# Second edge stage of a two-layer graph network: destination rows by spans of ranks instead of gathers

## What is computed

```
ms = src_s[edge_src] + dst_s[edge_dst]          # 64 scalars
mv = src_v[edge_src] + dst_v[edge_dst]          # 32 vectors of 3
w  = radial(edge_scalars) @ rw3 + roff          # 224 weights an edge, w1..w5
ds = [w1 * ms, w4 * (mv . Y1)]
dv = [(w2 * ms) Y1, w3 * mv, w5 * cross(mv, Y1)]
ls, lv = linear(ds), linear(dv)                 # 8 heads
a  = softmax over the edges of one destination of the heads' logits
ns, nv = segment sums of a * values by edge_dst
```

## Time and profile before

| | |
|---|---|
| median of 3 runs | 10502.52 us (10501.54 to 10524.19) |
| the profiled execution's own time | 10505.42 us |
| its span, first to last instruction | 10503.6 us |
| mean granted TensorE clock | 0.923 of full speed |
| PE, DVE, ACT, POOL busy over the span | 82%, 76%, 45%, 73% |
| layer1_edges, first to last sum (line 1849) | 5637.8 to 9768.5 us |

### The profile page before, as it was taken

One profiled execution on the slowest core, in us unless ns is written; L12 is line 12 of the kernel. 1 busy time (PEld: TensorE's weight loads), 2 busy tenths in 40 slices (PEclk: granted clock), 3 DMA queues, 4 the chain that ended last, 5 costly groups with the idle time before them and its releaser, 6 DMA issues. The chain is left out here.

```text
span 10503.6 us, 169632 instructions
## 1 busy us (share of the span) xinstructions
PE 8641.0 (82%) x31592; PEld 4931.7 (47%) x31592; DVE 7996.0 (76%) x15399; ACT 4717.1 (45%) x8484; POOL 7636.1 (73%) x5822
## 2 busy tenths in 40 slices
PE   0888888888888799999996888888888887788598
PEld 0444444444444232223233666666666665566333
DVE  3277777777777587888886888888888888888565
ACT  0177666666666311111112444444444444444255
POOL 4488888888888787777785777777777777777332
PEclk9599999999999899999997999999999999999699
DMA  5588888888888899999993444444444444444222
GB/s 202 177 169 168 166 167 166 169 164 172 165 167 168 180 231 225 228 226 229 228 226 90 136 138 136 135 133 139 136 135 135 136 140 135 133 135 137 71 76 58
DMA packets 1075659, 1661.68 MB, mean 158 GB/s; under 512 B 215917, under 2 KB 815288, under 8 KB 1019704
## 3 DMA queue, kind: packets, MB, share of 16 engines
q1 hardware_dynamic: 679744, 1199.16, 41.6%
q0 software_dynamic: 395520, 458.93, 24.5%
HBM read 1483.21 MB, written 443.97 MB: 183 GB/s over the span
## 5 line engine op out<-in xcount | busy, mean ns | idle before, releaser
L436 POOL DMA_INDIRECT sums<-e_total,e_place x1568 | 2481.9, 1583 | 586.3 <-DMA sums<-e_total,e_place 315.7
L1837 POOL DMA_INDIRECT e_rows<-TS,e_at x1568 | 1644.3, 1049 | 567.7 <-issue 451.4
L1837 POOL DMA_INDIRECT e_rows<-TD,e_at x1568 | 1537.3, 980 | 478.0 <-issue 478.0
L573 PE MATMUL ps<-e_win,e_pick 128*128 128x448 f32 x3136 | 1350.6, 576 | 152.9 <-DVE e_u L470 112.4
L1997 PE MATMUL ps<-w_r,e_h 128*128 128x224 f32 x3136 | 840.5, 420 | 424.6 <-DVE e_d L1880 376.1
L573 PEld LDWEIGHTS ps<-e_win,e_pick 128*128 128x128 f32 x3136 | 626.4, 205 | 920.0 <-issue 835.5
L1086 POOL TENSOR_TENSOR n_zv<-n_zv,n_ast 128x1536 f32<-128x1536 f32 x200 | 755.3, 3776 | 410.2 <-DMA n_zv<-in_x_groups 399.3
L1997 PEld LDWEIGHTS ps<-w_r,e_h 128*128 128x128 f32 x3136 | 659.2, 221 | 682.7 <-DVE e_d L1880 558.1
L2006 PE MATMUL ps<-ident,e_d 128*128 128x128 f32 x4704 | 683.6, 283 | 110.1 <-ACT e_dT L2114 108.6
L1266 PE MATMUL ps<-n_z,w_uss 128*64 128x512 f32 x1600 | 742.2, 607 | 26.5 <-DVE n_z L1109 25.8
L2114 ACT ACTIVATE e_oT<-ps 128x512 f32<-128x512 f32 x784 | 468.3, 597 | 628.3 <-PE ps L2032 488.5
(11 more groups left out here) (433 smaller groups left out, 18808.0 us busy)
## 6 DMA issues: line engine op xcount, KB each, us to landing
e_win<-T SPq DMA_DIRECT2D x1568, 168.0 KB
n_z<-in_x_groups SPq DMA_DIRECT2D x400, 512.0 KB
n_zv<-in_x_groups SPq DMA_DIRECT2D x800, 192.0 KB
TOT<-e_tot SPq DMA_DIRECT2D x392, 352.0 KB
e_row<-in_src_rows SPq DMA_DIRECT2D x98, 1024.0 KB
e_row<-in_dst_rows SPq DMA_DIRECT2D x98, 1024.0 KB
e_win<-T SPq DMA_DIRECT2D x1568, 56.0 KB
e_local<-LR SPq DMA_DIRECT2D x98, 512.0 KB
```

The lines of the kernel that those rows point to most:

```text
L436: pool.indirect_dma_start(sums[c], bass.IndirectOffsetOnAxis(ap=place[:, r % 4, c:c + 1], axis=0), total[:, r % 4, c, 0:MSG0], None, compu ...
L573: pe.matmul(g[:, c, :], pick[:, p, R * c:R * c + R], win[:, s, c, :], start=True, stop=True).then_inc(spread, 1)
L1837: pool.indirect_dma_start(rows[:, p, x, c, :], None, table, bass.IndirectOffsetOnAxis(ap=at[:, gp, x, col:col + 1], axis=0)).then_inc(rows ...
```

## The change

TD's rows are stored by rank, and layer1_edges reads them as layer0_edges reads T0: one window of 32 ranks a tile, or of 128 where the flag says so, spread to the edges by a matmul with a 0/1 selection, and copied from PSUM to the place in `rows` that the gather filled. Part by part:
- `edge_ranks` also writes first ranks and flags to a DRAM table BASE (one transfer); `node_ranks` clears 128 rows behind TD.
- `node_update0`: SyncE stores only TS; GpSimd copies four columns of ranks and issues two indirect scatters to TD behind each of the parts 6 and 7 of a group (100 in all).
- `layer1_edges`, GpSimd: four gathers a step instead of eight.
- SyncE: load_windows(i+4) ahead of each step's other work: 8 register loads and 8 transfers (4 of them conditional); every fourth step load_base and load_local (512 KB, LR to all partitions).
- VectorE: selections(i+3) as the last instruction of a step; sums waits for far_kept.
- TensorE: spread_out(i+2) in two halves, each of two matmuls with 160 columns, ahead of the halves of turn_back(i-1); turn_back comes ahead of weights(i+1).
- ScalarE: keep_far(i+2), two copies of 128x320, ahead of all else in a step.

The core of the diff:

```
-def layer1_edges(nc, m, k, ps, W, TS, TD, index, dstI, rows_dst, heads_dst, H, yx, TOT):
+def layer1_edges(nc, m, k, ps, W, TS, TD, index, LR, BASE, iota, dstI, rows_dst, heads_dst, H, yx, TOT):
...
         def bank(i, j):
-            return 2 + (5 * i.r + j) % 2
+            return 2 + (7 * i.r + j) % 2
...
+                def load_windows(i):
...
+                    for c in range(GT):
+                        sp.dma_start(win[0:FEW, s, c, :], TD[bass.ds(starts[c], FEW), :]).then_inc(win_here[s], 16)
+                        sp.dma_start(win[FEW:128, s, c, :], TD[bass.ds(starts[c] + FEW, 128 - FEW), :], cond=more[c]
+                                     ).then_inc(win_here[s], 16)
...
-                        for x, table in enumerate((TS, TD)):
-                            for c in range(GT):
-                                col = 4 * (r % 4) + c
-                                pool.indirect_dma_start(rows[:, p, x, c, :], None, table, bass.IndirectOffsetOnAxis(
-                                    ap=at[:, gp, x, col:col + 1], axis=0)).then_inc(rows_here[p][x], 16)
+                        for c in range(GT):
+                            col = 4 * (r % 4) + c
+                            pool.indirect_dma_start(rows[:, p, 0, c, :], None, TS, bass.IndirectOffsetOnAxis(
+                                ap=at[:, gp, col:col + 1], axis=0)).then_inc(rows_here[p], 16)
...
+                    dve.tensor_scalar(pick[:, p, :], local[:, gp, GT * R * s:GT * R * s + GT * R], iota[:, 0:1], None,
+                                      ALU.is_equal).then_inc(picked, 1)
...
                         if not i.before(5):
                             members(i)
+                        if i.plus(3).within():
+                            selections(i.plus(3))
...
+                def spread_out(i, half, to, after):
+                    p, s = i.r % 2, i.r % 4
+                    if half == 0:
+                        gate(pe, k)
+                        pe.wait_ge(picked, i.n(1, 1))
+                        gate(pe, k)
+                        pe.wait_ge(win_here[s], i.uses(256, 128 * (i.r // 4) + 128))
+                    if after is not None:
+                        gate(pe, k)
+                        pe.wait_ge(*after)
+                    for c in (2 * half, 2 * half + 1):
+                        last = pe.matmul(to[:, c % 2], pick[:, p, R * c:R * c + R], win[:, s, c, :], start=True, stop=True)
+                    last.then_inc(spread, 1)
...
+                        if i.plus(2).within():
+                            spread_out(i.plus(2), 0, far2(i, 0), (far_kept, 3) if i.before(1) else (kept, i.n(5, -1)))
+                        if not i.before(1):
+                            turn_back(i.plus(-1), 0)
+                        if i.plus(2).within():
+                            spread_out(i.plus(2), 1, far2(i, 1), (far_kept, 4) if i.before(1) else (kept, i.n(5)))
+                        if not i.before(1):
+                            turn_back(i.plus(-1), 1)
                         if not (isinstance(t, int) and t == PASSES - 1 and r == STEPS - 1):
                             weights(after)
-                        if not i.before(1):
-                            turn_back(i.plus(-1), 0)
-                            turn_back(i.plus(-1), 1)
...
+                def keep_far(i, half, of):
+                    gate(act, k)
+                    act.wait_ge(spread, i.n(2, half + 1))
+                    if half == 0 and not i.before(2):
+                        gate(act, k)
+                        act.wait_ge(added, i.n(1, 1, 2))
+                    act.activation(rows[:, i.r % 2, 1, 2 * half:2 * half + 2, :], of, ACT.Copy).then_inc(far_kept, 1)
...
                         i = At(t, r)
+                        if i.plus(2).within():
+                            keep_far(i.plus(2), 0, far2(i, 0))
+                            keep_far(i.plus(2), 1, far2(i, 1))
                         if r % 4 == 1 and not i.before(5):
                             weigh_up(i)
                         if not i.before(1):
```

In node_update0:

```
-                    for j, to in enumerate((TS, TD)):
-                        sp.dma_start(to[at, :].rearrange("(t n) w -> n t w", t=2), rows[:, r, :, X * j:X * j + X]
-                                     ).then_inc(stored[r], 16)
+                    sp.dma_start(TS[at, :].rearrange("(t n) w -> n t w", t=2), rows[:, r, :, 0:X]).then_inc(stored[r], 16)
...
+                    for j in range(2):
+                        pool.indirect_dma_start(TD, bass.IndirectOffsetOnAxis(ap=rank_of[:, c.p, 2 * r + j:2 * r + j + 1], axis=0),
+                                                rows[:, r, j, X:2 * X], None).then_inc(placed[r], 16)
...
+                        if s >= 6 and not g.before(1):
+                            place(g.plus(-1), s - 6)
```

More of the change, by code:

```diff
@@ L160, in _, with edge_ranks @@
                 dve.wait_ge(cast, len(casts))
-def edge_ranks(nc, m, k, ps, dstI, before, lower, LR, baseI):
+def edge_ranks(nc, m, k, ps, dstI, before, lower, LR, baseI, BASE):
     own = ExitStack()
@@ L230, in _, with node_ranks @@
                                    ).then_inc(kept, 1)
-def node_ranks(nc, m, k, ps, P, lower, nodes, T0):
+def node_ranks(nc, m, k, ps, P, lower, nodes, T0, TD):
     own = ExitStack()
@@ L940, in groups, with node_update0 @@
         body(Group(0, 0).plus(i))
-def node_update0(nc, m, k, ps, W, xT, xG, sums, X1, TS, TD):
+def node_update0(nc, m, k, ps, W, xT, xG, sums, X1, TS, TD, rank):
     own = ExitStack()
@@ L960, in node_update0 @@
         rows = sb("n1_rows", [128, 2, 2, 2 * X])
+        rank_of = sb("n1_rank_of", [128, 2, 4], I32)
+        ranked, begun = sem("n1_ranked"), sem("n1_begun")
+        placed = [sem(f"n1_placed{r}") for r in range(2)]
         x_here, ag_here = [sem(f"n1_x_here{p}") for p in range(2)], sem("n1_ag_here")
@@ L1090, in vectors, with ranks, place @@
                         pool.tensor_tensor(zv[:, b, 0], zv[:, b, 0], zv[:, b, i], ALU.add).then_inc(zv_ready, 1)
+                def ranks(c):
+                    if not c.before(2):
+                        for r in range(2):
+                            gate(pool, k)
+                            pool.wait_ge(placed[r], c.n(32, 0, 1))
+                    pool.tensor_copy(rank_of[:, c.p], rank[:, bass.ds(c.n(4), 4)]).then_inc(ranked, 1)
+                def place(c, r):
+                    gate(pool, k)
+                    pool.wait_ge(rows_kept, c.n(2, r + 1))
+                    gate(pool, k)
+                    pool.wait_ge(ranked, c.n(1, 1))
+                    pool.sem_inc(begun, 1)
+                    gate(pool, k)
+                    for j in range(2):
+                        pool.indirect_dma_start(TD, bass.IndirectOffsetOnAxis(ap=rank_of[:, c.p, 2 * r + j:2 * r + j + 1], axis=0),
+                                                rows[:, r, j, X:2 * X], None).then_inc(placed[r], 16)
                 def body(g):
@@ L1096, in body @@
                             add_up(g.plus(1))
+                        if s == 4 and not g.before(1):
+                            ranks(g.plus(-1))
+                        if s >= 6 and not g.before(1):
+                            place(g.plus(-1), s - 6)
                 add_up(Group(0, 0))
                 groups(pool, body)
+                ranks(Group(NG // 2, 0))
+                for r in range(2):
+                    place(Group(NG // 2, 0), r)
             @block.vector
@@ L1787, in body @@
                     for r in range(STEPS):
-                        i = At(t, r)
+                        i, ahead = At(t, r), At(t, r).plus(4)
+                        if ahead.within():
+                            gate(sp, k)
+                            sp.wait_ge(spread, ahead.n(2, 2, 4))
+                            load_windows(ahead)
+                        if r % 4 == 0 and not final:
+                            load_base(r // 4, t + 1)
+                        if r % 4 == 1 and not final:
+                            gate(sp, k)
+                            sp.wait_ge(picked, i.n(1, 3))
+                            load_local(r // 4, t + 1)
                         if not (final and r >= 6):
@@ L1809, in _ @@
                 for p in range(2):
+                    load_base(p, 0)
+                    load_local(p, 0)
                     load_at(p, 0)
                     load_h(p, 0)
+                sp.wait_ge(blank, 1)
+                for r in range(4):
+                    load_windows(At(0, r))
                 for p in range(2):
@@ L1975, in _ @@
                 dve.wait_ge(ones_set, 2)
+                for r in range(3):
+                    selections(At(0, r))
                 sums(At(0, 0))
@@ L1998, in weights @@
                     last.then_inc(w_ready, 1)
+                def spread_out(i, half, to, after):
[11 more added lines that the diff above has]
+                    last.then_inc(spread, 1)
                 def turn(i, j):
                     p = i.r % 2
```

(19 more changed lines are left out.)

84 lines of the change are left out of this document (64 added, 20 removed).

## The result

The changed kernel takes 10873.17 us (median of 4 runs, 10863.72 to 10891.59), the kernel before beside it 10502.03 us (4 runs, 10497.09 to 10524.19): ratio 1.0356, 95% interval 1.0332 to 1.0379, slower by 371 us. The profiled execution took 10891.59 us with a span of 10889.8, 386.2 us more than the span before.

The account below looks back on a forecast made before the run. GpSimd's gather queue was taken as the limit, VectorE close behind. New waits make a group 44.6 us against 42.3, +226 us; node_update0 +10 and prologue +5 give +241, forecast 10745 us, range 10420 to 10950.

Parts of the forecast that it names:

- the forecast's own case: Whole kernel: slower through new waits in the second edge stage, 10680 to 10880 us, chance 0.42.
- rival 4: Behind the scans TensorE stays at its lower clock, or SyncE binds: +400 to +600 us, 10900 to 11100; chance 0.11.
- What bounds before, the floor: Second edge stage: GpSimd's queue sets the pace by a little; without other VectorE waits a changed group takes 40.4 us.
- plain step: Second edge stage, VectorE step without scans or new wait: 9.00 us plus a selection of 0.48, 9.48 us.
- The scan step: Second edge stage, one step in four: forward scan waits 1.06 us for logits_up, so the step takes 12.98 us.
- The step behind the scans, order: ScalarE's Exp and table loads stand behind keep_far: 2.54 us of new VectorE wait, step 12.02 us.
- P: The end of VectorE's selection, which releases TensorE's spreads; VectorE starts its next step then too.
- The step behind the scans, clock: TensorE, idle some 3.5 us, may run at its lower clock: 0 to 1.2 us a group, 0.6 taken.
- node_update0: Four scatters a group of 512 nodes, covered by GpSimd's waits for transfers: +10 us taken, 125 without cover.
- The rest: BASE and the longer prologue: 0 to 15 us, 5 taken.
- SyncE: Windows and register loads in the edge stage: 0 taken, upper bound 0.7 us a step, 270 us.
- rival 5: Selections and gathers exclude each other, 0.95 us lost a selection: 372 us more, 11120 us; chance 0.02.

Follow-up runs that it names:

- e5: The kernel before without its gathers of destination rows, nothing in their place: 10224.03 us, beside the kernel before at 12677.2 us.
- e4: The changed kernel with selections first on VectorE, and Exp and turned-back results ahead of the spread rows: 10419.26 us, ratio to the kernel before 0.9927.
- e6: The changed kernel with five unread matmuls added on TensorE behind the logits' weighting: 10750.87 us, ratio to the kernel before 1.0235; 11400.18 under the other condition.
- the last two sets: Two of four sets of experiment runs, each with the kernel before alongside; there it took 10506.19 and 10503.86 us.
- the first two: The two earlier sets of experiment runs, each with the kernel before alongside; there it took 12677.2 and 12687.29 us.
- e1: The changed kernel with the selection for step i+3 moved from last to first in VectorE's step: 10589.76 us, ratio 1.0082; 10876.67 under the other condition.
- e3: The changed kernel with selections first on VectorE and Exp ahead of ScalarE's two copies: 10458.96 us, ratio 0.9955; 10791.59 and 10785.89 under the other condition.
- the first set: The earliest of four sets of experiment runs, four altered kernels with the kernel before alongside at 12677.2 us.

## Why the prediction was right, and where its size was off

Slower was forecast with 0.70, at 10745 us (+241 on the profiled execution), and 10873 us was measured (+386 by the spans): the forecast's own case, at its upper end (10680 to 10880), just short of rival 4, the clock (10900 and more). By its own steps:

- **What bounds before, the floor.** GpSimd's queue was the limit by a little: confirmed in that with half of the gathers VectorE waits for no row, and e5, the kernel before with that alone changed, has a group of 39.3 us instead of 42.2. The floor of 40.4 us a group stands: e4 has 40.3 in the second group of a pass. The terms are right to 0.1 us (plain step 9.48 forecast, 9.38 measured, as a selection costs 0.40 from start to start, not its duration of 0.48).
- **The scan step.** Forecast 12.98 us with 1.06 of wait for logits_up; measured 13.09 with 1.05. But only in the second group of each pass (33 waits in 65 groups): in the first VectorE itself comes 1.3 us late to the pass ("issue"), and the step is 11.97. The forecast counted this wait for all 98 groups; that the late start fills its place in the other 49 is luck.
- **The step behind the scans, order.** Forecast without the clock: results at P + 6.25, step 12.02. e6, which has TensorE at full clock, has P + 6.52 and 12.23. Right, 0.2 short.
- **The step behind the scans, clock: the step that failed.** I took 0.6 us, half-way between the bounds of 0 and 1.2. It is 13.78 - 12.23 = 1.55 us, above my upper bound. The forecast's own terms had it: 0.57 + 0.43 + 0.57 = 1.57 us of TensorE stand ahead of the second copy, and at 0.50 they take as much again; the copy is at P + 3.60 against P + 2.04, 1.56 us later. The rows of a single weight group led me to less, and the half for idle time "between the rows with and without it" was wrong too: from P to P + 4 us the mean granted clock was at most 0.71 behind all 94 scans of the 47 inner passes; in e6 it was 1.00 behind 93 of them. Times 98, that is 0.95 x 98 = 93 us of the 145 that the forecast lacks.
- **The first group of a pass.** The forecast summed one kind of group. The first one is 46.2 us in the mean, the second 45.5: the start of a pass costs VectorE 1.3 us and its scan step saves 1.1, but its last step is 0.5 longer, by a wait for ScalarE's results that e6 mostly lacks. Half the difference, over 98 groups, is 31 us.
- **The stage's account.** The four steps of a second group are 1.06 us over the forecast together (clock 0.95, order 0.2, scan step 0.1, the two plain steps -0.2), 104 us over 98 groups; with the 31 of the first groups that is 135. The stage missed the forecast by 340.7 - 226 = 115 us; the 20 between lie at the ends of the stage and between medians and means.
- **node_update0.** Forecast +10, measured +11.8 in this pair of profiles. The same code was profiled eleven times in kernels made from the change and three times in the kernel before, e5 among them: from the first to the last n_z it took 1990 to 2027 us (mean 2011) and 1987 to 1996 (mean 1992), so +19 is the better figure. The cover was the one named: GpSimd's wait for transfers fell from 327.7 us to 96.4, while the 100 scatters take 998 ns each at the median.

```profile
POOL n_zv L1094 <- DMA n_zv<-in_x_groups: 96.4, 28, 10.5
L1115 POOL DMA_INDIRECT TD<-n_rows,n_rank_of x100: 960/998/2522, 3719.8 to 5620.7; - x100
```

- **The rest.** Forecast 5, measured 34.0 in this pair, most of it in layer0_edges, whose code is the same. Over the same fourteen profiles the first n_z comes at 3554 to 3582 us (mean 3563) instead of 3541 to 3548 (mean 3544), so some 19 of the 27.4 us are the kernel's and the others scatter. GpSimd's indirect adds take 1552 ns at the median in all eleven and 1542 in all three: 1568 x 0.010 = 16 us if each delay is passed on, which is argued, not shown. Why each takes 10 ns more was not tried.

```profile
L442 POOL DMA_INDIRECT sums<-e_total,e_place x1568: 1547/1552/2083, 504.2 to 3540.2; - x196
```

- **SyncE.** Taken at 0, with up to 0.7 us a step. Its waits of 506.0 and 460.3 us leave 3.7 us a step free: 0 was right.
- **Selections beside gathers** (rival 5). The selections of the new stage are between 474 and 631 ns, median 481, but they hardly test the rival: by their starts and ends only 4 of 392 overlap a gather, as the gathers follow the sums at the start of a step. The first edge stage tests it: there 387 of 392 selections overlap an indirect add of 1.55 us and 357 begin inside one, at a median of 478 ns and at most 819. By the rule that the prediction cites (Trainium skill, SBUF — State Buffer, section Who interferes with whom), a selection in a two-port mode that came second would wait for the whole of the other instruction. None waits out an add; whether these selections run in such a mode no run shows.

```profile
L492 DVE TENSOR_SCALAR e_pick<-e_local,nodes_sb x392: 361/478/819, 475.9 to 3494.6; 128x512 f32<-128x512 bf16 x196
L1937 DVE TENSOR_SCALAR e_pick<-e_local,nodes_sb x392: 474/481/631, 5676.2 to 10142.5; 128x512 f32<-128x512 bf16 x196
```

- **Signs.** I named GpSimd at "about 45%" of the stage: it is 34%, as the 0.30 us between gathers are not counted as busy. The Exp's table load did run behind keep_far, and the steps came at 11.44 us.

## What to carry to other kernels

When work is moved to engines that have room, its place in their queues decides, not the room: here two matmul groups and two copies were put ahead of work on the path, released by the last instruction of another engine's step, and that cost 4.9 us of a group of 46, while the change without its new waits is worth 1.2 (e5's gain of 2.9 from the gathers, less four selections). Ask of each added item what stands behind it, put it there behind what is awaited sooner, and make what releases it a step early. Where a stretch of idle TensorE lies ahead of the path, and rows of such a stretch show the lower clock behind it, price all the matmuls that follow on the path at the lower clock (here 1.57 us of them), not one instruction.

## What was not expected of the hardware

- The same program took 10502 to 10506 us in the result and in the last two sets, and 12677 to 12697 us in the first two; the change is 3.6% slower under the first of these conditions and 9.0% faster under the second. The second edge stage begins within 3 us of the same time under both conditions for the kernel before and for the change (within 15 for e1 and 51 for e3). In that stage TensorE ends its matmuls late in stretches (3.50 us for four transposes, 0.437 elsewhere).
- The kernels were hit very unequally: the kernel before by 2183 us, the change by 679, e3 by 327. Which trait of a kernel brings the stretches on is open: e5, with the kernel before's TensorE program and half of its gathers, took 10224 us. No run tells whether the cause lies in the chip or around it; the record has the number 15 for the chip of the first set (12677 us) and of the last (10504 us), so the condition need not stay with a chip.
- A TensorE kept busy with five matmuls a group that nobody reads gained 1.1% (10873 to 10751 us).
